# Moving half of the second corner sums of a deformable convolution from Pool to DVE

## The chip, the cores and the metric

The kernel runs on one core of a Trainium2 chip. The metric is the device time of one execution in microseconds, as the median of several runs.

PE is TensorE, DVE is VectorE, ACT is ScalarE, Pool is GpSimd, SP is the engine that issues the loads.

## What is computed

The reference is a chain of eight residual blocks on a tensor x of shape (8, 64, 16, 16), all in float32: multi-scale linear attention, a mixture of experts with two experts per token, a deformable convolution, a feed-forward layer on half of the tokens, a state-space scan along rows, a batch-norm mixture of experts, an involution, and a mixture of experts with one expert per token and a capacity. Each block's input is normalised over channels or tokens.

The change is in the deformable convolution. Two 3x3 convolutions give an offset for each of 4 channel groups and 9 taps, 36 samples per pixel. Each sample is interpolated between four corner pixels, and one product with the weights sums over groups, channels and taps:

```python
val = gather(y0, x0) * (wy0 * wx0)[:, :, None] + gather(y0, x0 + 1) * (wy0 * wx1)[:, :, None] \
    + gather(y0 + 1, x0) * (wy1 * wx0)[:, :, None] + gather(y0 + 1, x0 + 1) * (wy1 * wx1)[:, :, None]
return jnp.einsum('ogck,bgckhw->bohw', wr, val)
```

and `x = x + relu(deform_conv(...))`.

## The kernel before, in words

The kernel holds x in SBUF from start to end and runs the blocks as stages, one after another. Inside a stage each engine has its own instruction list, written out by hand, and semaphores tie the lists together: an instruction increments one when it is done, another engine waits until it has reached a number. The stage of the deformable convolution stands at lines 950 to 1293.

The 2048 pixels (8 images of 256) are 16 tiles of 128 partitions. After the offsets are known, the stage loops over the 36 samples. For one sample `s`:

- SP loads the sample's pixel indices, broadcast to 128 partitions, into one of four buffers `BC` (L1002), as soon as DVE and ACT have used the buffer's former content.
- DVE compares them with the partition's own number (`compare`, L1261), which gives the one-hot matrix `OH` for the lower half of an image. ACT makes `OHU` for the upper half (L1184). Both have three buffers.
- PE gathers the four corners by 64 matmuls with these matrices (`gather`, L1079) into two of four banks of PSUM, alternating with s. It waits for both matrices and, for the bank, for DVE's product of sample s - 2.
- DVE multiplies the gathered corners by the interpolation weights (`weigh`, L1271, two instructions of 128x512) into `U[s % 2]`, which is the tile SQ for even and SD for odd samples. It waits for the gather, and for Pool to be done with `U` of sample s - 2. This pair of instructions is called the product of s.
- Pool adds corners 0 and 1 to corners 2 and 3 (L1015, the first sum, into `V1`) and then the two halves of that (L1018, the second sum, into `VAL`). Samples 0 to 34 are done so; for sample 35 DVE makes both sums itself (L1284, L1285).

DVE's order in the loop is: comparison of s + 1, then product of s. So a comparison runs one sample ahead of its product.

`VAL` has two buffers of eight samples each. When eight samples are summed, PE transposes them (`contract`, L1100, 16 matmuls in four groups, each evicted by ACT, L1177) and later multiplies them by the weights (`project`, L1113). Both stand in PE's list between gathers: `contract` after the gathers of samples 11, 19, 27 and 34, `project` after those of 15, 23 and 31. After the gather of sample 35 follow the last `project` of a full group, the contraction of the last four samples, and their projection. DVE's two last instructions of the stage (L1293) add the result to x.

Pool's loop and DVE's product, with what they wait for:

```python
pool.wait_ge(u_ready, s + 1)
after_pool(pool, pool.tensor_tensor(V1[:, :, :, :], U[s % 2][:, :, 0:2, :], U[s % 2][:, :, 2:4, :], ALU.add))
...
pool.tensor_tensor(VAL[:, (s // 8) % 2, :, s % 8, :], V1[:, :, 0, :], V1[:, :, 1, :], ALU.add).then_inc(val_ready, 1)
pool.wait_ge(val_ready, s + 1)
...
dve.wait_ge(ga_ps, s + 1)
if s >= 2:
    dve.wait_ge(val_ready, s - 1)
```

Three other stages (the mixtures of experts) compute a softmax of gate logits (`softmax_dve`, L736) and use semaphores `g_ps`, `g_exp` and `g_sum` for it, each stage its own three.

Of the kernel before, what the change touches and what calls it, by code (L numbers as in the profile page):

```python
# [12 lines left out]
ALU = mybir.AluOpType  # L13
ACT = mybir.ActivationFunctionType
F32 = mybir.dt.float32
# [5 lines left out]
P = 128  # L21
# [5 lines left out]
TILES = B * PIX // P  # L27
# [7 lines left out]
SAMPLES = 36  # L35
CG = 16
# [39 lines left out]
def build(nc, x_dram, packs, idx_dram, out_dram):  # L76
    with ExitStack() as ctx:
        def sb(name, shape, dt=F32, where=None):
            return (where or ctx).enter_context(nc.sbuf_tensor(name, shape, dt))

        def sem(name):
            return ctx.enter_context(nc.semaphore(name))
# [14 lines left out]
        def wt(name, a=0, n=None, p0=0, p1=P):  # L97
# [10 lines left out]
            "ln_centered", "ln_squared", "ln_var", "ln_sd", "ln_rstd", "ln_spread", "ln_placed", "ln_copied", "ln_done"))  # L108
        TILED = (2, 4, 5)
        dve_step = sem("dve_step")  # L110
        act_step = sem("act_step")
# [18 lines left out]
        def after_pool(eng, ins):  # L130

            steps["pool"] += 1
            ins.then_inc(pool_step, 1)
            eng.wait_ge(pool_step, steps["pool"])
# [115 lines left out]
        with ExitStack() as sctx, nc.Block() as block:  # L250
# [17 lines left out]
            for s in range(1, SCALES):  # L268
# [6 lines left out]
            prepared, ones_set, qkv_ps, qkv_in, t_ps, t_act, t_dve, conv_ps, conv_in, d5_ready, d3_ready = (  # L275
                sem(n) for n in ("prepared", "ones_set", "qkv_ps", "qkv_in", "t_ps", "t_act", "t_dve", "conv_ps", "conv_in",
                                 "d5_ready", "d3_ready"))
# [484 lines left out]
        with ExitStack() as sctx, nc.Block() as block:  # L762
# [11 lines left out]
            HS = sb("HS", [P, 4, HC], F32, sctx)  # L774
            g_ps, g_exp, g_sum, cw_ready, cwt_ps, cwt_in, hid_ps, hid_in, bc_ps, hs_ready, hs_used, cwt3_act, cwt3_dve, cast0, cwt3_ps = (
                sem(n) for n in ("g_ps", "g_exp", "g_sum", "cw_ready", "cwt_ps", "cwt_in", "hid_ps", "hid_in",
                                 "bc_ps", "hs_ready", "hs_used", "cwt3_act", "cwt3_dve", "cast0", "cwt3_ps"))
# [159 lines left out]
        with ExitStack() as sctx, nc.Block() as block:  # L937
# [30 lines left out]
            U = [a[:, :].rearrange("p (t k c) -> p t k c", t=TILES, k=4) for a in (SQ, SD)]  # L968
            V1 = sb("V1", [P, TILES, 2, CG], F32, sctx)
            VAL = sb("VAL", [P, 2, TILES, 8, CG], F32, sctx)  # L970
# [4 lines left out]
                "val_ready", "vt_ps", "vt_in", "dc_ps", "xs_ready"))  # L975
            vt_dve, wc_ready, last_val = sem("s3_vt_dve"), sem("s3_wc_ready"), sem("s3_last_val")

# [29 lines left out]
            @block.gpsimd  # L1007
            def _(pool):
                pool.memset(YP[:, :, :], 0.0).then_inc(y_pad, 1)
                for k in range(3):  # L1010
                    pool.memset(HS3[k][:, :, :], 0.0).then_inc(y_pad, 1)
                for s in range(SAMPLES - 1):

                    pool.wait_ge(u_ready, s + 1)
                    after_pool(pool, pool.tensor_tensor(V1[:, :, :, :], U[s % 2][:, :, 0:2, :], U[s % 2][:, :, 2:4, :], ALU.add))  # L1015
                    if s >= 16 and s % 8 == 0:
                        pool.wait_ge(vt_ps, 4 * (s // 8 - 1))
                    pool.tensor_tensor(VAL[:, (s // 8) % 2, :, s % 8, :], V1[:, :, 0, :], V1[:, :, 1, :], ALU.add).then_inc(val_ready, 1)  # L1018
                    pool.wait_ge(val_ready, s + 1)

            @block.tensor
            def _(pe):
# [60 lines left out]
                def contract(ch):  # L1083

                    ns = min(8, SAMPLES - 8 * ch)
                    rows = ns * CG
                    pe.wait_ge(val_ready, min(8 * ch + ns, SAMPLES - 1))
                    if ch == 4:
                        pe.wait_ge(last_val, 1)
                    for j, q in enumerate(LAST if ch == 4 else range(4)):  # L1090
                        n = 4 * ch + j
                        if n == 19:
                            pe.wait_ge(vt_dve, 1)
                        elif n >= 2:
                            pe.wait_ge(vt_in, n - 1)
                        for i in range(4):

                            t = 4 * (2 * (q % 2) + i // 2) + 2 * (q // 2) + i % 2
                            src = VAL[:, ch % 2, t, 0:ns, :].rearrange("p s c -> p (s c)")
                            mm = pe.transpose(bank(j % 2)[0:rows, i * P:(i + 1) * P], src, wt("ident"))  # L1100
                        mm.then_inc(vt_ps, 1)
                    return rows
# [91 lines left out]
            def _(dve):  # L1194
# [62 lines left out]
                def compare(s):  # L1257
                    dve.wait_ge(bc_in[s % NBC], 16 * (s // NBC + 1))
                    if s >= NOH:
                        dve.wait_ge(ga_ps, s - NOH + 1)  # L1260
                    dve.tensor_scalar(OH[:, s % NOH, :], BC[:, s % NBC, :], wt("qidx"), 0.0625, ALU.is_equal, ALU.mult).then_inc(oh_ready, 1)  # L1261

                def weigh(s):
                    dve.wait_ge(ga_ps, s + 1)
                    if s >= 2:
                        dve.wait_ge(val_ready, s - 1)
                    for half in range(2):
                        o = U[s % 2][:, 8 * half:8 * half + 8, :, :].rearrange("p t k c -> p (t k) c")
                        src = bank(4 + 2 * (s % 2) + half).rearrange("p (k c) -> p k c", c=CG)
                        w = WC[:, s, 8 * half:8 * half + 8, :].rearrange("p t (k o) -> p (t k) o", o=1).broadcast_to([P, 32, CG])  # L1270
                        ins = dve.tensor_tensor(o, src, w, ALU.mult)  # L1271
                    ins.then_inc(u_ready, 1)

                compare(0)
                compare(1)
                dve.wait_ge(wc_ready, NB)
                for s in range(SAMPLES):
                    if 1 <= s < SAMPLES - 1:
                        compare(s + 1)
                    weigh(s)  # L1280
                last = SAMPLES - 1
                sums = PY[:, :, :].rearrange("p t k -> p (t k)")[:, 0:TILES * 2 * CG].rearrange("p (t k c) -> p t k c", k=2, c=CG)
                dve.wait_ge(u_ready, last + 1)
                after(dve, dve.tensor_tensor(sums, U[last % 2][:, :, 0:2, :], U[last % 2][:, :, 2:4, :], ALU.add))  # L1284
                dve.tensor_tensor(VAL[:, (last // 8) % 2, :, last % 8, :], sums[:, :, 0, :], sums[:, :, 1, :], ALU.add).then_inc(last_val, 1)  # L1285
                for j in (1, 3):
# [194 lines left out]
        with ExitStack() as sctx, nc.Block() as block:  # L1481
# [14 lines left out]
            H2W = sb("H2W", [P, H2WBUF, HC], F32, sctx)  # L1496
            (bn_sd, bn_done, sum_done, g_ps, g_exp, g_sum, g_ready, wt_ps, wt_in, wb_ps, wb_in, a_ps, a_in, b_ps, b_in, weighted,
             c_done) = (sem("s6_" + n) for n in (
                "bn_sd", "bn_done", "sum_done", "g_ps", "g_exp", "g_sum", "g_ready", "wt_ps", "wt_in", "wb_ps", "wb_in", "a_ps",
                "a_in", "b_ps", "b_in", "weighted", "c_done"))  # L1500
# [103 lines left out]
            def _(act):  # L1604
# [31 lines left out]
                relu1(1)  # L1636
                act.wait_ge(g_exp, 1)
                act.activation(LG[:, :, :], LG[:, :, :], ACT.Exp).then_inc(g_sum, 1)
# [12 lines left out]
            def _(dve):  # L1651
# [4 lines left out]
                for i in range(2):  # L1656
# [9 lines left out]
                dve.tensor_reduce(SUM[:, :], Y[:, :].rearrange("p (b n) -> p n b", b=NB), AX.X, ALU.add).then_inc(sum_done, 1)  # L1666
                dve.wait_ge(g_ps, 1)
                br = wt("br2").rearrange("p (o e) -> p o e", o=1).broadcast_to([P, 2, E])
                after(dve, dve.scalar_tensor_tensor(out=LG[:, :, :], in0=bank(0, 2 * E).rearrange("p (h e) -> p h e", h=2),
                                                    scalar=1.0 / B, in1=br, op0=ALU.mult, op1=ALU.add))  # L1670
                softmax_dve(dve, LG, RED, 2, g_exp, 1, g_sum)
                dve.wait_ge(lg_zeroed, 1)
# [217 lines left out]
        with ExitStack() as sctx, nc.Block() as block:  # L1890
# [17 lines left out]
            oht_ps, oht_in, x_final = sem("s8_oht_ps"), sem("s8_oht_in"), sem("s8_x_final")  # L1908
            (g_ps, g_exp, g_sum, oh_ready, cum_ps, t_ps, t_in, scale_ready, sc_ps, sc_in, hid_ps, hid_in_a, hid_in_v,
             hid_used) = (sem("s8_" + n) for n in (  # L1910
                "g_ps", "g_exp", "g_sum", "oh_ready", "cum_ps", "t_ps", "t_in", "scale_ready", "sc_ps", "sc_in",
                "hid_ps", "hid_in_a", "hid_in_v", "hid_used"))
# [27 lines left out]
            def _(pe):  # L1940
# [24 lines left out]
                up_w(0)  # L1965
                pe.wait_ge(g_exp, 1)
                up_w(2)
# [63 lines left out]
            def _(act):  # L2031
# [3 lines left out]
                act.wait_ge(ln_done, 16)  # L2035
                act.wait_ge(g_exp, 1)
                act.activation(LG[:, :, :], LG[:, :, :], ACT.Exp).then_inc(g_sum, 1)
# [24 lines left out]
            def _(dve):  # L2062
                ln_dve(dve, 7, flat)
                dve.wait_ge(w_in[8], W_AT[8])
                dve.wait_ge(g_ps, 1)
                for bh in range(2):
# [3 lines left out]
                after(dve, ins)  # L2070
                softmax_dve(dve, LG, RED, TILES, g_exp, 1, g_sum)
                first_max_dve(dve, LG, OTHERS, RED, OH8)
# [307 lines left out]
```

## Time and profile before

| | us |
|---|---|
| median of 3 runs | 561.73 (558.81 to 562.38) |
| the profiled execution | 558.03 |
| its span, from first to last instruction | 556.0 |
| deformable stage, product of sample 0 to product of sample 35 | 226.10 to 317.85 |

The span lies 2.0 us below the profiled execution's own time. The mean granted clock of TensorE over the span is 0.975 of full speed. All rows are of that one execution. A group line of the page has the engine, the operation, the tile written and the tiles read, the shape, the count, then the busy time in us and the mean duration of one instruction in ns, then the idle time of the engine just before these instructions and what ended most of it.

### The profile page before, as it was taken

The numbers are of one execution on the slowest core, as the hardware profiler recorded it, in microseconds if no ns is written. First come the engines' busy times: TensorE is split into PE (matmuls) and PEld (weight loads), VectorE is DVE, ScalarE is ACT, GpSimd is POOL, SyncE is SP. The second block draws the span as 40 slices with busy tenths as digits, with TensorE's granted clock in tenths as the row PEclk, the third lists the DMA queues.
The fourth block names the chain that finished last, engine by engine and source line by source line (L and its number), as shares of the span: only waits on it lengthen the run. The fifth ranks groups of instructions, "written<-read, shape, count | busy, mean of one in ns | idle before, by whom it ended". The sixth has DMA issues, their size and how long they took to land. (4 is left out here: it accounts for less than half of the span.)

```text
span 556.0 us, 12345 instructions
## 1 busy us (share of the span) xinstructions
PE 490.4 (88%) x5281; PEld 253.3 (46%) x5281; DVE 345.6 (62%) x590; ACT 279.6 (50%) x405; POOL 132.0 (24%) x129
## 2 busy tenths in 40 slices
PE   3799998978997999879999979897988898999994
PEld 1344323635222496778888743332324255333331
DVE  2385997467557267677777658666557564763534
ACT  2583223535552136978788447556771552433330
POOL 8080000000003000699999900006102001000000
PEclk9999999998999799999999999988999899999998
DMA  7000000020000002755556000101003000000000
GB/s 290 2 2 2 1 2 1 1 105 6 1 0 34 1 2 93 261 205 212 198 196 212 19 19 2 64 0 46 1 0 123 1 2 2 1 1 0 1 19 19
DMA packets 7990, 29.83 MB, mean 54 GB/s; under 512 B 864, under 2 KB 2176, under 8 KB 7424
## 3 DMA queue, kind: packets, MB, share of 16 engines
q1 hardware_dynamic: 7936, 29.05, 15.0%
q8 instruction: 41, 0.67, 0.5%
q14 instruction: 13, 0.11, 0.1%
HBM read 28.37 MB, written 0.67 MB: 52 GB/s over the span
## 5 line engine op out<-in xcount | busy, mean ns | idle before, releaser
L1079 PE MATMUL PS<-GX,OH 128*128 128x64 f16 x1152 | 70.0, 193 | 9.1 <-DVE OH L1261 9.1
L1184 ACT ACTIVATE OHU<-BC,wbuf 128x2048 fp8e4<-128x2048 f16 x36 | 70.2, 1995 | 11.2 <-PE PS L1079 7.1
L1079 PEld LDWEIGHTS PS<-GX,OH 128*128 128x128 f16 x1152 | 67.5, 98 | 14.0 <-DVE OH L1261 10.4
L1079 PE MATMUL PS<-GX,OHU 128*128 128x64 f16 x1152 | 69.9, 193 | 0.0
L1079 PEld LDWEIGHTS PS<-GX,OHU 128*128 128x128 fp8e4 x1152 | 67.5, 98 | 0.0
L2162 DVE TENSOR_SCALAR HID<-PS,wbuf 128x512 f32<-128x512 f32 x32 | 23.9, 750 | 31.3 <-PE PS L1954 26.4
L2052 ACT ACTIVATE HID<-PS,wbuf 128x512 f32<-128x512 f32 x32 | 21.9, 687 | 39.8 <-PE PS L1954 39.8
L1018 POOL TENSOR_TENSOR VAL<-V 128x256 f32<-128x256 f32 x35 | 40.2, 1147 | 2.7
L695 DVE SCALAR_TENSOR_TENSOR D<-QKVP,wbuf,D 128x1024 f32<-128x1024 f32 x27 | 34.6, 1281 | 7.7 <-ACT D L595 6.9
L426 PE MATMUL PS<-T,DG 128*32 128x512 f32 x336 | 37.1, 594 | 0.0
L1947 PE MATMUL PS<-Y,wbuf 64*128 64x512 f32 x128 | 35.6, 617 | 0.7 <-ACT HID L2052 0.6
L1015 POOL TENSOR_TENSOR V<-SQ 128x512 f32<-128x512 f32 x18 | 24.4, 1354 | 49.6 <-DVE SQ L1271 48.3
L1271 DVE TENSOR_TENSOR SQ<-PS,WC 128x512 f32<-128x512 f32 x36 | 23.2, 686 | 15.1 <-POOL VAL L1018 7.7
L2010 PE MATMUL PS<-HID,wbuf 128*64 128x512 f32 x128 | 30.8, 604 | 0.0
L156 PE MATMUL PS<-X,wconst 128*128 128x512 f32 x32 | 17.4, 671 | 14.4 <-DMA wconst<-pack_dram 7.5
L1271 DVE TENSOR_TENSOR SD<-PS,WC 128x512 f32<-128x512 f32 x36 | 23.2, 684 | 10.7 <-POOL VAL L1018 9.0
L1261 DVE TENSOR_SCALAR OH<-BC,wbuf 128x2048 f16<-128x2048 f16 x36 | 27.9, 774 | 2.0 <-DMA BC<-idx_dram 2.0
L930 DVE TENSOR_TENSOR HS<-PS,HID 128x512 f32<-128x512 f32 x32 | 20.6, 686 | 13.5 <-PE PS L809 13.4
L875 ACT ACTIVATE HID<-PS,wbuf 128x512 f32<-128x512 f32 x32 | 20.2, 684 | 13.4 <-PE PS L800 13.4
L184 ACT ACTIVATE SQ<-PS 128x512 f32<-128x512 f32 x16 | 9.6, 597 | 33.5 <-PE PS L156 25.5
L595 ACT ACTIVATE D<-PS,wbuf 128x512 f32<-128x512 f32 x12 | 8.3, 688 | 28.6 <-PE PS L426 28.6
L800 PE MATMUL PS<-Y,wbuf 64*128 64x512 f32 x64 | 20.7, 689 | 1.5 <-ACT HID L875 1.5
(313 smaller groups left out, 917.0 us busy)
## 6 DMA issues: line engine op xcount, KB each, us to landing
BC<-idx_dram SPq DMA_DIRECT2D x36, 512.0 KB, 4.4
wbuf<-pack_dram SPq DMA_DIRECT2D x1, 1913.0 KB, 9.5
wbuf<-pack_dram SPq DMA_DIRECT2D x1, 1656.0 KB, 7.5
wbuf<-pack_dram SPq DMA_DIRECT2D x1, 1494.0 KB, 6.1
wbuf<-pack_dram SPq DMA_DIRECT2D x1, 1044.0 KB, 11.5
wbuf<-pack_dram SPq DMA_DIRECT2D x1, 871.0 KB, 4.5
wbuf<-pack_dram SPq DMA_DIRECT2D x1, 607.0 KB, 5.4
X<-x_dram SPq DMA_DIRECT2D x2, 256.0 KB, 4.2
```

The lines of the kernel that those rows point to most:

```text
L426: mm = pe.matmul(bank(DBANK[t % 2] + n)[32 * q:32 * q + 32, :], DG[:, (2 * j + hf) * NBLK + i, :], src, start=(i == blocks[0]), stop=(i == ...
L695: ins = dve.scalar_tensor_tensor(out=d, in0=window(QKVP[j], dy, dx), scalar=wt("dw5", j * 25 + 5 * dy + dx, 1), in1=d, op0=ALU.mult, op1=A ...
L1015: after_pool(pool, pool.tensor_tensor(V1[:, :, :, :], U[s % 2][:, :, 0:2, :], U[s % 2][:, :, 2:4, :], ALU.add))
L1018: pool.tensor_tensor(VAL[:, (s // 8) % 2, :, s % 8, :], V1[:, :, 0, :], V1[:, :, 1, :], ALU.add).then_inc(val_ready, 1)
L1079: mm = pe.matmul(o, (OH, OHU)[qh][:, s % NOH, t * P:(t + 1) * P], src, start=(qh == 0 and part == 0), stop=(qh == 1 and part == 1))
L1184: act.activation(OHU[:, s % NOH, :], BC[:, s % NBC, :], ACT.Abs_reciprocal_sqrt, bias=wt("hitq"), scale=HIT, saturate=False).then_inc(uppe ...
L1261: dve.tensor_scalar(OH[:, s % NOH, :], BC[:, s % NBC, :], wt("qidx"), 0.0625, ALU.is_equal, ALU.mult).then_inc(oh_ready, 1)
L1271: ins = dve.tensor_tensor(o, src, w, ALU.mult)
L1947: pe.matmul(bank(2 + (n + bh) % 4), wt("w1_3", e * FH3 + m * P, P, r, r + C), Y[r:r + C, bp * HC:(bp + 1) * HC], start=True, stop=False, t ...
L2010: pe.matmul(bank(bp)[C * bh:C * bh + C, :], wt("w2_3", (2 * e + m) * C, C), HID[:, (n + i) % 8, :], start=(e == 0 and m == 0), stop=(e == ...
L2052: act.activation(HID[:, n % 8, :], bank(2 + n % 4), ACT.Relu, bias=wt("b1_3", 2 * e + m, 1)).then_inc(hid_in_a, 1)
L2162: dve.tensor_scalar(HID[:, n % 8, :], bank(2 + n % 4), wt("b1_3", 2 * e + m, 1), 0.0, ALU.add, ALU.max).then_inc(hid_in_v, 1)
```

## The change

For odd samples 1 to 33 the second sum moves from Pool to DVE (`corner_sum`). DVE does the one of sample s - 2 between the comparison of s + 1 and the product of s, for odd s. Pool keeps all first sums and the second sums of even samples. `V1` becomes two buffers, by the sample's parity, and gets a semaphore of its own, `v1_ready`; DVE's product of s waits for it (first sum of s - 2) instead of `val_ready`. DVE's second sums count on `val_dve`, for which Pool waits before it writes the odd `V1` again. The contractions wait for both counters, half the number of samples each. The sample 35 counts on `val_dve` too, and `last_val` goes.

To make room for the new semaphores, the three mixture stages share one set of `g_ps`, `g_exp` and `g_sum`, and wait for 1, 2 and 3 in turn.

```diff
-            V1 = sb("V1", [P, TILES, 2, CG], F32, sctx)
+            V1 = sb("V1", [P, 2, TILES, 2, CG], F32, sctx)
+            v1_ready, val_dve = sem("s3_v1_ready"), sem("s3_val_dve")
...
                 for s in range(SAMPLES - 1):
 
                     pool.wait_ge(u_ready, s + 1)
-                    after_pool(pool, pool.tensor_tensor(V1[:, :, :, :], U[s % 2][:, :, 0:2, :], U[s % 2][:, :, 2:4, :], ALU.add))
+                    if s >= 3 and s % 2:
+                        pool.wait_ge(val_dve, s // 2)
+                    pool.tensor_tensor(V1[:, s % 2, :, :, :], U[s % 2][:, :, 0:2, :], U[s % 2][:, :, 2:4, :], ALU.add).then_inc(v1_ready, 1)
+                    if s % 2:
+                        continue
+                    pool.wait_ge(v1_ready, s + 1)
                     if s >= 16 and s % 8 == 0:
                         pool.wait_ge(vt_ps, 4 * (s // 8 - 1))
-                    pool.tensor_tensor(VAL[:, (s // 8) % 2, :, s % 8, :], V1[:, :, 0, :], V1[:, :, 1, :], ALU.add).then_inc(val_ready, 1)
-                    pool.wait_ge(val_ready, s + 1)
+                    pool.tensor_tensor(VAL[:, (s // 8) % 2, :, s % 8, :], V1[:, 0, :, 0, :], V1[:, 0, :, 1, :], ALU.add).then_inc(val_ready, 1)
+                    pool.wait_ge(val_ready, s // 2 + 1)
...
-                    pe.wait_ge(val_ready, min(8 * ch + ns, SAMPLES - 1))
-                    if ch == 4:
-                        pe.wait_ge(last_val, 1)
+                    pe.wait_ge(val_ready, (8 * ch + ns) // 2)
+                    pe.wait_ge(val_dve, (8 * ch + ns) // 2)
...
                 def weigh(s):
                     dve.wait_ge(ga_ps, s + 1)
                     if s >= 2:
-                        dve.wait_ge(val_ready, s - 1)
+                        dve.wait_ge(v1_ready, s - 1)
...
+                def corner_sum(s):
+                    dve.wait_ge(v1_ready, s + 1)
+                    if s >= 16 and s % 8 == 1:
+                        dve.wait_ge(vt_ps, 4 * (s // 8 - 1))
+                    dve.tensor_tensor(VAL[:, (s // 8) % 2, :, s % 8, :], V1[:, 1, :, 0, :], V1[:, 1, :, 1, :], ALU.add).then_inc(val_dve, 1)
+
...
                     if 1 <= s < SAMPLES - 1:
                         compare(s + 1)
+                    if s >= 3 and s % 2:
+                        corner_sum(s - 2)
                     weigh(s)
...
-                dve.tensor_tensor(VAL[:, (last // 8) % 2, :, last % 8, :], sums[:, :, 0, :], sums[:, :, 1, :], ALU.add).then_inc(last_val, 1)
+                dve.tensor_tensor(VAL[:, (last // 8) % 2, :, last % 8, :], sums[:, :, 0, :], sums[:, :, 1, :], ALU.add).then_inc(val_dve, 1)
...
-                dve.wait_ge(g_ps, 1)
+                dve.wait_ge(g_ps, 2)
...
-                softmax_dve(dve, LG, RED, 2, g_exp, 1, g_sum)
+                softmax_dve(dve, LG, RED, 2, g_exp, 2, g_sum)
```

## Rows read from the trace of the kernel before

**Rows 1.** The page's costliest groups: PE, ACT and DVE in the stage.

```profile
L1079 PE MATMUL PS<-GX,OH 128*128 128x64 f16 x1152 | 70.0, 193 | 9.1 <-DVE OH L1261 9.1
L1184 ACT ACTIVATE OHU<-BC,wbuf 128x2048 fp8e4<-128x2048 f16 x36 | 70.2, 1995 | 11.2 <-PE PS L1079 7.1
...
L1271 DVE TENSOR_TENSOR SQ<-PS,WC 128x512 f32<-128x512 f32 x36 | 23.2, 686 | 15.1 <-POOL VAL L1018 7.7
...
L1271 DVE TENSOR_TENSOR SD<-PS,WC 128x512 f32<-128x512 f32 x36 | 23.2, 684 | 10.7 <-POOL VAL L1018 9.0
```

**Rows 2.** Busy time by stretch: from:to, length, engines (instructions), clock, DMA share, GB/s.

```profile
257.37:278.41 21.04, 19.48 (x543) 17.37 (x539) 15.85 (x25) 17.64 (x13) 19.79 (x17) 1.00 0.60 203
```

The engines of Rows 2 stand in the order PE matmul, PE weight load, DVE, ACT, Pool.

**Rows 3.** Timeline of Pool: start, duration, line, operation, tiles, shapes, count.

```profile
227.47 1.71 POOL L1015 TENSOR_TENSOR V<-SQ 128x512 f32<-128x512 f32 x1 [48.26 <-DVE SQ L1271]
...
251.74 1.28 POOL L1015 TENSOR_TENSOR V<-SD 128x512 f32<-128x512 f32 x1
253.09 1.21 POOL L1018 TENSOR_TENSOR VAL<-V 128x256 f32<-128x256 f32 x1
254.38 1.28 POOL L1015 TENSOR_TENSOR V<-SQ 128x512 f32<-128x512 f32 x1
...
258.37 0.73 POOL L1018 TENSOR_TENSOR VAL<-V 128x256 f32<-128x256 f32 x1
259.18 1.60 POOL L1015 TENSOR_TENSOR V<-SQ 128x512 f32<-128x512 f32 x1
...
318.36 0.74 POOL L1018 TENSOR_TENSOR VAL<-V 128x256 f32<-128x256 f32 x1
```

**Rows 4.** Timeline of DVE; a product's two instructions are one line.

```profile
226.10 1.29 DVE L1271 TENSOR_TENSOR SQ<-PS,WC 128x512 f32<-128x512 f32 x2 [2.27 <-PE PS L1079]
227.30 0.74 DVE L1261 TENSOR_SCALAR OH<-BC,wbuf 128x2048 f16<-128x2048 f16 x1
227.96 1.28 DVE L1271 TENSOR_TENSOR SD<-PS,WC 128x512 f32<-128x512 f32 x2
...
251.76 1.29 DVE L1271 TENSOR_TENSOR SQ<-PS,WC 128x512 f32<-128x512 f32 x2 [0.70 <-POOL VAL L1018]
...
254.40 1.29 DVE L1271 TENSOR_TENSOR SD<-PS,WC 128x512 f32<-128x512 f32 x2 [0.69 <-POOL VAL L1018]
...
257.37 1.29 DVE L1271 TENSOR_TENSOR SQ<-PS,WC 128x512 f32<-128x512 f32 x2 [1.01 <-PE PS L1079]
258.57 1.08 DVE L1261 TENSOR_SCALAR OH<-BC,wbuf 128x2048 f16<-128x2048 f16 x1
...
317.85 1.29 DVE L1271 TENSOR_TENSOR SD<-PS,WC 128x512 f32<-128x512 f32 x2 [1.68 <-PE PS L1079]
...
319.90 0.42 DVE L1285 TENSOR_TENSOR VAL<-PY 128x256 f32<-128x256 f32 x1
```

**Rows 5.** Timeline of PE: first matmuls of gathers, a contraction and a projection.

```profile
251.12 0.23 PE L1079 MATMUL PS<-GX,OH 128*128 128x64 f16 x2 [0.60 <-DVE OH L1261]
...
253.00 1.07 PE L1100 MATMUL PS<-wconst,VAL 128*128 128x128 f32 x8
...
255.30 0.22 PE L1079 MATMUL PS<-GX,OH 128*128 128x64 f16 x2
...
259.71 0.23 PE L1079 MATMUL PS<-GX,OH 128*128 128x64 f16 x2 [0.52 <-DVE OH L1261]
...
263.55 1.94 PE L1113 MATMUL PS<-VTA,wbuf 128*64 128x512 f32 x8
265.42 0.23 PE L1079 MATMUL PS<-GX,OH 128*128 128x64 f16 x2
```

**Rows 6.** Timelines of a later stage: Pool's scalings, and two additions on DVE.

```profile
383.51 2.92 POOL L1518 TENSOR_SCALAR DGI<-wconst,wbuf 128x128 f32<-128x128 f32 x5
...
384.27 0.21 DVE L739 TENSOR_TENSOR LG<-LG,RED 128x16 f32<-128x16 f32 x1
...
385.16 0.17 DVE L743 TENSOR_TENSOR LG<-LG,RED 128x16 f32<-128x16 f32 x1
```

More of the change, by code:

```diff
@@ L109, in build @@
         TILED = (2, 4, 5)
+        g_ps, g_exp, g_sum = (sem(n) for n in ("g_ps", "g_exp", "g_sum"))
         dve_step = sem("dve_step")
@@ L774, in build @@
             HS = sb("HS", [P, 4, HC], F32, sctx)
-            g_ps, g_exp, g_sum, cw_ready, cwt_ps, cwt_in, hid_ps, hid_in, bc_ps, hs_ready, hs_used, cwt3_act, cwt3_dve, cast0, cwt3_ps = (
-                sem(n) for n in ("g_ps", "g_exp", "g_sum", "cw_ready", "cwt_ps", "cwt_in", "hid_ps", "hid_in",
+            cw_ready, cwt_ps, cwt_in, hid_ps, hid_in, bc_ps, hs_ready, hs_used, cwt3_act, cwt3_dve, cast0, cwt3_ps = (
+                sem(n) for n in ("cw_ready", "cwt_ps", "cwt_in", "hid_ps", "hid_in",
                                  "bc_ps", "hs_ready", "hs_used", "cwt3_act", "cwt3_dve", "cast0", "cwt3_ps"))
@@ L975, in build @@
                 "val_ready", "vt_ps", "vt_in", "dc_ps", "xs_ready"))
-            vt_dve, wc_ready, last_val = sem("s3_vt_dve"), sem("s3_wc_ready"), sem("s3_last_val")
+            vt_dve, wc_ready = sem("s3_vt_dve"), sem("s3_wc_ready")
             bc_in = [sem(f"bc_in{i}") for i in range(NBC)]
@@ L1496, in build @@
             H2W = sb("H2W", [P, H2WBUF, HC], F32, sctx)
-            (bn_sd, bn_done, sum_done, g_ps, g_exp, g_sum, g_ready, wt_ps, wt_in, wb_ps, wb_in, a_ps, a_in, b_ps, b_in, weighted,
+            (bn_sd, bn_done, sum_done, g_ready, wt_ps, wt_in, wb_ps, wb_in, a_ps, a_in, b_ps, b_in, weighted,
              c_done) = (sem("s6_" + n) for n in (
-                "bn_sd", "bn_done", "sum_done", "g_ps", "g_exp", "g_sum", "g_ready", "wt_ps", "wt_in", "wb_ps", "wb_in", "a_ps",
+                "bn_sd", "bn_done", "sum_done", "g_ready", "wt_ps", "wt_in", "wb_ps", "wb_in", "a_ps",
                 "a_in", "b_ps", "b_in", "weighted", "c_done"))
@@ L1636, in _ @@
                 relu1(1)
-                act.wait_ge(g_exp, 1)
+                act.wait_ge(g_exp, 2)
                 act.activation(LG[:, :, :], LG[:, :, :], ACT.Exp).then_inc(g_sum, 1)
@@ L1908, in build @@
             oht_ps, oht_in, x_final = sem("s8_oht_ps"), sem("s8_oht_in"), sem("s8_x_final")
-            (g_ps, g_exp, g_sum, oh_ready, cum_ps, t_ps, t_in, scale_ready, sc_ps, sc_in, hid_ps, hid_in_a, hid_in_v,
+            (oh_ready, cum_ps, t_ps, t_in, scale_ready, sc_ps, sc_in, hid_ps, hid_in_a, hid_in_v,
              hid_used) = (sem("s8_" + n) for n in (
-                "g_ps", "g_exp", "g_sum", "oh_ready", "cum_ps", "t_ps", "t_in", "scale_ready", "sc_ps", "sc_in",
+                "oh_ready", "cum_ps", "t_ps", "t_in", "scale_ready", "sc_ps", "sc_in",
                 "hid_ps", "hid_in_a", "hid_in_v", "hid_used"))
@@ L1965, in _ @@
                 up_w(0)
-                pe.wait_ge(g_exp, 1)
+                pe.wait_ge(g_exp, 3)
                 up_w(2)
@@ L2035, in _ @@
                 act.wait_ge(ln_done, 16)
-                act.wait_ge(g_exp, 1)
+                act.wait_ge(g_exp, 3)
                 act.activation(LG[:, :, :], LG[:, :, :], ACT.Exp).then_inc(g_sum, 1)
@@ L2064, in _ @@
                 dve.wait_ge(w_in[8], W_AT[8])
-                dve.wait_ge(g_ps, 1)
+                dve.wait_ge(g_ps, 3)
                 for bh in range(2):
@@ L2070, in _ @@
                 after(dve, ins)
-                softmax_dve(dve, LG, RED, TILES, g_exp, 1, g_sum)
+                softmax_dve(dve, LG, RED, TILES, g_exp, 3, g_sum)
                 first_max_dve(dve, LG, OTHERS, RED, OH8)
```

## The prediction

> **What bounds the kernel now.** I read the page's costliest groups first [rows 1]. In the deformable stage (lines 950 to 1293) the engines run side by side, and two groups of waits stand out: DVE's products (L1271) wait 7.7 + 9.0 = 16.7 us for Pool's second corner sums, and PE's gathers (L1079) wait 9.1 us for DVE's comparisons. Next I read the stage as stretches of time [rows 2]: from the product of sample 12 to that of sample 20, one round of eight samples in 21.04 us, Pool is busy 19.79 us and PE 19.48 us, at a granted clock of 1.00. Two engines are nearly full, so relieving one may only uncover the other.
>
> Pool's timeline [rows 3] gives the present pace. A first sum (128x512) takes 1.28 us, then come 0.07 us, a second sum (128x256) of 1.21 us and 0.08 us: 254.38 - 251.74 = 2.64 us a sample. DVE's products keep exactly that pace (251.76, 254.40) [rows 4]. A second sum's own work is only 0.73 us (258.37; also 318.36); the other 0.48 us is a comparison on DVE that it runs into. It works the other way too: the comparison at 258.57 began 0.20 us into the second sum of 258.37 and took 1.08 instead of 0.74 us, ending at 259.65, 0.55 us after that sum. And the first sum issued at 259.18 took 1.60 us, ending 1.13 us after that comparison. So Pool's sums and DVE's comparisons exclude each other, in both directions [rows 3, 4].
>
> PE's rows [rows 5] give the rest. A gather begins 0.06 us after its comparison (259.65, then 259.71) and holds PE 253.00 - 251.12 = 1.88 us; the product follows 2.07 us behind the gather's start (255.30, then 257.37). A contraction holds PE 255.30 - 253.00 = 2.30 us, a projection 265.42 - 263.55 = 1.87 us.
>
> **The change part by part.** Removed: 17 second sums of Pool (odd samples 1 to 33), 17 x 1.21 = 20.6 us of Pool's time; and DVE's product of sample s now waits for the first sum of s - 2 alone. Added: 17 second sums on DVE, queued behind a comparison and ahead of a product. The row for it is DVE's own last second sum, 0.42 us (319.90) [rows 4]. The next instruction starts some 0.07 us before such an end (227.96, where the comparison ends at 228.04), which leaves 0.35 us each. The new waits of Pool (for DVE's earlier second sum) and of the contractions (for both counters) are met early: DVE's sum of s - 2 stands ahead of the product of s, for which Pool waits anyway, and the contractions come two or more samples behind the sums they read. They cost nothing; were one late by a whole sum, 0.42 us, the four contractions would lose 1.7 us. The doubled buffer lets an odd first sum be followed at once by the next one. The gate counters shared by other stages change the numbers that are waited for, and no order: nothing.
>
> How the stage then runs I follow through one pair, from the product of an even sample e at time 0 (us):
> - 1.20: DVE begins the comparison of e + 2 (226.10, then 227.30 [rows 4]); it ends at 1.94. Pool's first sum of e, whose products are ready at 1.29, is held by it and ends 1.13 later, at 3.07.
> - 1.86: DVE's corner sum of e - 1 (0.66 after the comparison's start: 227.30, 227.96). 2.21: the product of e + 1. 3.41: the comparison of e + 3.
> - 3.15 to 3.88: Pool's second sum of e. The comparison of e + 3 begins 0.26 us into it, as the one at 258.57 began 0.20 into its own, and so ends 0.55 behind it, at 4.43. The next product starts 0.08 us earlier: the pair takes 4.35.
>
> Pool has 3.3 us of its own work in those 4.35 and bounds nothing. What is late next is a loop that Pool had covered: product, comparison, gather, product two samples on. It takes 1.20 + 0.74 + 0.06 + 2.07 = 4.07 us for two samples with no collision; DVE's own work in a pair (2 x 1.20 + 2 x 0.66 + 0.35 = 4.07) is as long. With the collision it is 4.35, against 5.29 now. 17 such pairs lie between the products of samples 1 and 35.
>
> But in that loop PE's other work no longer hides. At present a gather (251.12) would allow its product at 253.19, and that starts at 254.40; a contraction shows merely as a wait of 1.01 in place of 0.70 us (257.37) [rows 4]. In the new pair the gather of e + 1 holds PE from 0.14 to 2.02 and that of e + 2 from 2.02; its product could start at 4.09 and does at 4.35. A contraction (after samples 11, 19 and 27) moves that gather to 4.32 and the product to 6.39, 2.04 us late; a projection (after 15, 23 and 31) moves them to 3.89 and 5.96, 1.61 late. After sample 34 the gather of 35 waits for a contraction: 2.02 + 1.88 + 2.30 + 2.07 = 8.27 against 6.56, 1.71 late. Together 3 x 2.04 + 3 x 1.61 + 1.71 = 12.7 us. So a round of eight is 4 pairs and 3.65 us, about as long as today, and what is gained is gained ahead of the first contraction. ScalarE (17.64 us busy in a round) and the index loads (0.60 of the DMA engines) [rows 2] have room at that pace.
>
> Does DVE's new sum, with both inputs in SBUF, exclude Pool's sums as a comparison does? No row shows that shape beside Pool. The nearest is an addition with two such inputs that DVE ran while Pool was in the midst of a scaling [rows 6]: 0.21 us, and 0.17 us for the same shape later, so 0.04 us of harm. Five scalings fill 2.92 us from 383.51; the second ends near 384.69, and the addition had ended at 384.48. That is no wait for Pool's instruction to end. I take 0.04 us a pair, as this row is the nearest; the ends are nothing, and a wait for a whole first sum, the second rival.
>
> The Trainium skill speaks against this value. "SBUF — State Buffer", section "Who interferes with whom", says that a DVE instruction with two SBUF inputs contends with a GpSimd instruction that reads SBUF, and that whichever comes second is blocked until the first is done; by it the pair would be 5.09 us. The 0.21 us of that row does not bear out a full block, though at 16 elements it is short and doesn't refute the rule.
>
> **The sum.** 17 x (4.35 + 0.04) = 74.6; plus 12.7; plus 0.4 for the first pair, where Pool's first sum collides at its start (1.71 us [rows 3]): 87.7 us from the product of sample 1 to that of sample 35, where it is now 317.85 - 227.96 = 89.9 [rows 4]. What follows the last product doesn't change. The gain is 2.2 us: 558.03 becomes 555.8 for the profiled execution. The median of the runs, 561.73, lies 3.7 above that; with the same gain it becomes **559.5 us**. The forecast's own range is 558 (the products of rows 3 to 5 with a few hundredths less in each pair) to 563.4 (Pool's and DVE's reads take turns: 256 elements at the pace of the 0.42 us sum, some 0.27 us a pair, so 17 x 0.23 more).
>
> **Rivals.**
> - **Pool's full gain.** If only DVE's work counted and PE's contractions and projections stayed hidden, 17 x 4.07 = 69.2, a gain of 20 us: 541. For it: Pool is the engine that products wait for. Against it: rows 5, by which the loop has no room for that work of PE's.
> - **Blocked corner sums, the slower side.** Place: DVE's corner sum, issued at 1.86, when Pool's first sum, waiting since 1.37, has just been let in. If it must wait for that one's end at 3.07, it ends at about 3.30, the product of e + 1 starts at 3.23, the comparison of e + 3 at 4.43 (no collision), the next product at 5.09. A contraction then costs 1.30 and a projection 0.87, the last contraction nothing: 17 x 5.09 + 3 x 2.17 + 0.4 = 93.4, 3.5 us slower: 565.2. It decides from a wait of about 0.5 us in every pair on. For it: comparisons and Pool's sums do exclude each other [rows 3, 4]. Against it: rows 6.
> - **No collision.** If the comparison of e + 3 comes ahead of Pool's second sum (0.26 us must shift), the pair is 4.07, and with no slack PE's work is added whole: 69.2 + 3 x (2.30 + 1.87) + 1.9 + 0.4 = 84.0, a gain of 5.9: 555.8. Against it: Pool's first sum hangs on the comparison before it, so the order repeats in every pair.
>
> **How the numbers follow.** Forecast 0.56, blocked sums 0.25, no collision 0.14, Pool's full gain 0.03, anything else on the slower side 0.02. A measurement of this kernel tells a change from none at about 1%, 5.6 us. Faster by more: the full gain and most of "no collision", 0.16 with a little of the forecast. Slower by more: "blocked" lies at 0.6%; half of that case and the rest may come out beyond, 0.17. Within 1%: 0.67. The range is 555.5 to 567: "no collision" at the low end, "blocked" and some 2 us that the order of the two engines may add at the high end.
>
> **What would show it.** Pool's busy time in the stage falls by about 17 us. Before the first contraction products come in pairs of about 4.4 us (5.1 if blocked, 4.1 without collision), and every second comparison takes about 1.05 us. The waits of products for Pool vanish and waits for PE take their place, over 2 us behind a contraction. A corner sum of over 1 us on DVE means the block. If rounds of eight samples fall below 19 us, the loop is not the bound, and this prediction is wrong.

## The result, and the profile after

The changed kernel took 568.84 us in the median of four runs (565.43 to 570.15), the kernel before 561.57 beside it: a ratio of 1.0148, with a 95% interval of 1.0109 to 1.0186. Ratios here and below leave out executions in a slower state and can differ a little from the quotient of the two medians, here 1.013. The forecast was 559.5 with a range of 555.5 to 567.0. It was on the wrong side and out of its range. Two later measurements of the same kernel (below) gave 1.0051 and 1.0073, so part of the 1.5% didn't repeat.

First, the profiled execution by stretch, before and after; the columns are those of [rows 2], and the third line of each is the time from the product of sample 1 to that of sample 35. The kernel before:

```profile
14.00:28.00 14.00, 11.21 (x108) 5.50 (x115) 4.35 (x6) 7.10 (x11) 1.17 (x2) 1.00 0.01 2
28.00:227.96 199.96, 185.00 (x1646) 90.46 (x1630) 132.87 (x223) 90.31 (x150) 17.22 (x18) 0.97 0.08 27
227.96:317.85 89.89, 80.59 (x2266) 73.07 (x2268) 66.42 (x103) 72.42 (x49) 84.56 (x69) 1.00 0.52 180
317.85:556.00 238.15, 208.38 (x1251) 82.52 (x1251) 138.79 (x257) 106.36 (x190) 17.28 (x27) 0.96 0.06 18
```

The kernel after (gathers now stand at L1086, first sums at L1019, Pool's second sums at L1025, comparisons at L1267, products at L1277, DVE's new sums at L1284):

```profile
14.00:28.00 14.00, 11.25 (x44) 5.80 (x52) 2.95 (x3) 5.39 (x8) 1.07 (x2) 0.76 0.00 1
28.00:230.27 202.27, 186.90 (x1710) 90.94 (x1710) 134.61 (x226) 91.96 (x153) 17.22 (x18) 0.98 0.08 26
230.27:324.59 94.32, 80.83 (x2266) 73.19 (x2268) 86.66 (x119) 72.10 (x49) 71.79 (x53) 1.00 0.50 172
324.59:568.00 243.41, 214.83 (x1251) 84.00 (x1251) 138.70 (x257) 106.42 (x190) 16.62 (x26) 0.94 0.05 17
```

Samples 1 to 35 take 94.32 us, 4.43 more than before, at a granted clock of 1.00 in both. (The one other profile with the stage of before, that of the additions beside scalings below, has 89.86 us.) Pool is relieved there by 12.8 us, DVE gets 20.2 more. The other 7.6 us of the two spans (568.0 and 556.0) lie outside: 2.3 ahead of sample 1 and 5.3 behind sample 35, where the change has no work beyond the renumbered gate counters, and where the granted clock was lower in places (0.76 against 1.00 from 14 to 28 us).

The costliest groups of the page after, against [rows 1]:

```profile
L1086 PE MATMUL PS<-GX,OH 128*128 128x64 f16 x1152 | 70.2, 193 | 13.3 <-DVE OH L1267 11.5
...
L1019 POOL TENSOR_TENSOR V<-SD 128x512 f32<-128x512 f32 x17 | 27.5, 1616 | 12.2 <-DVE SD L1277 12.1
...
L1277 DVE TENSOR_TENSOR SQ<-PS,WC 128x512 f32<-128x512 f32 x36 | 23.1, 682 | 8.2 <-PE PS L1086 8.2
...
L1284 DVE TENSOR_TENSOR VAL<-V 128x256 f32<-128x256 f32 x17 | 24.4, 1433 | 0.0
L1277 DVE TENSOR_TENSOR SD<-PS,WC 128x512 f32<-128x512 f32 x36 | 23.0, 677 | 1.4 <-PE PS L1086 1.4
```

The products' 16.7 us of waits for Pool are gone, and now Pool waits for DVE (12.1 us). The line that differs from the forecast is L1284: 17 corner sums fill 24.4 us of DVE, where the forecast had 17 x 0.46 (0.42 and 0.04 of harm). Their timeline on DVE, columns as in [rows 4]:

```profile
239.11 0.74 DVE L1267 TENSOR_SCALAR OH<-BC,wbuf 128x2048 f16<-128x2048 f16 x1
239.77 1.49 DVE L1284 TENSOR_TENSOR VAL<-V 128x256 f32<-128x256 f32 x1
241.18 1.27 DVE L1277 TENSOR_TENSOR SD<-PS,WC 128x512 f32<-128x512 f32 x2
242.38 0.74 DVE L1267 TENSOR_SCALAR OH<-BC,wbuf 128x2048 f16<-128x2048 f16 x1
243.04 1.28 DVE L1277 TENSOR_TENSOR SQ<-PS,WC 128x512 f32<-128x512 f32 x2
...
259.69 1.29 DVE L1277 TENSOR_TENSOR SQ<-PS,WC 128x512 f32<-128x512 f32 x2 [1.18 <-PE PS L1086]
...
322.73 0.42 DVE L1284 TENSOR_TENSOR VAL<-V 128x256 f32<-128x256 f32 x1
324.59 1.29 DVE L1277 TENSOR_TENSOR SD<-PS,WC 128x512 f32<-128x512 f32 x2 [1.44 <-PE PS L1086]
```

And on Pool, against [rows 3]:

```profile
239.27 1.71 POOL L1019 TENSOR_TENSOR V<-SQ 128x512 f32<-128x512 f32 x1
241.05 0.80 POOL L1025 TENSOR_TENSOR VAL<-V 128x256 f32<-128x256 f32 x1
...
322.83 1.45 POOL L1019 TENSOR_TENSOR V<-SQ 128x512 f32<-128x512 f32 x1
```

Pool's first sum is issued at 239.27, into the comparison that ends at 239.85, and ends 1.13 later (240.98), as in [rows 3]. DVE's corner sum, issued at 239.77, is by then the second in line: it ends at 241.26, 0.28 behind Pool's sum, and has taken 1.49 us for work of 0.42. The last corner sum has no comparison ahead of it and is issued 0.10 us before Pool's first sum (322.73, 322.83). Then the roles change: it takes 0.42 us, and Pool's sum takes 1.45, ending at 324.28, again 1.13 behind the end of DVE's instruction. So the two exclude each other, and the first one in keeps the other out. The total agrees: 16 x 1.50 + 0.42 = 24.4.

A pair of samples takes 3.27 + 1.86 = 5.13 us (237.91 to 243.04 on DVE). That is no more than the 2 x 2.64 us before. The loss shows where PE has other work, which Pool's pace had hidden: a pair with a contraction takes 6.38 us (253.31 to 259.69), one with a projection 6.05, so 1.25 and 0.92 us more, three times each. 17 x 5.13 + 3 x 2.17 makes 93.7 of the 94.3 us.

### The profile page after: what moved, and what is told of

The parts are those of the page before. It is cut to its first block and busy times, and to the rows that moved or that the text cites. A ratio compares the mean times of both kernels' runs of the same rounds, so it can differ in the third digit from the quotient of the medians.

```text
span 568.0 us, 12332 instructions
## 1 busy us (share of the span) xinstructions
PE 498.5 (88%) x5281; PEld 255.5 (45%) x5281; DVE 365.8 (64%) x607; ACT 279.2 (49%) x405; POOL 118.6 (21%) x112
## 5 line engine op out<-in xcount | busy, mean ns | idle before, releaser
L1086 PE MATMUL PS<-GX,OH 128*128 128x64 f16 x1152 | 70.2, 193 | 13.3 <-DVE OH L1267 11.5
L1086 PEld LDWEIGHTS PS<-GX,OH 128*128 128x128 f16 x1152 | 67.5, 98 | 18.3 <-DVE OH L1267 13.6
L1086 PE MATMUL PS<-GX,OHU 128*128 128x64 f16 x1152 | 70.1, 193 | 0.0
L1086 PEld LDWEIGHTS PS<-GX,OHU 128*128 128x128 fp8e4 x1152 | 67.5, 98 | 0.0
L1019 POOL TENSOR_TENSOR V<-SQ 128x512 f32<-128x512 f32 x18 | 30.6, 1698 | 57.2 <-DVE SQ L1277 55.9
L1961 PE MATMUL PS<-Y,wbuf 64*128 64x512 f32 x128 | 36.5, 632 | 0.7 <-ACT HID L2066 0.6
L157 PE MATMUL PS<-X,wconst 128*128 128x512 f32 x32 | 19.1, 728 | 14.7 <-DMA wconst<-pack_dram 7.7
L1019 POOL TENSOR_TENSOR V<-SD 128x512 f32<-128x512 f32 x17 | 27.5, 1616 | 12.2 <-DVE SD L1277 12.1
L1267 DVE TENSOR_SCALAR OH<-BC,wbuf 128x2048 f16<-128x2048 f16 x36 | 27.0, 749 | 2.4 <-DMA BC<-idx_dram 2.4
L1277 DVE TENSOR_TENSOR SQ<-PS,WC 128x512 f32<-128x512 f32 x36 | 23.1, 682 | 8.2 <-PE PS L1086 8.2
L1284 DVE TENSOR_TENSOR VAL<-V 128x256 f32<-128x256 f32 x17 | 24.4, 1433 | 0.0
L1277 DVE TENSOR_TENSOR SD<-PS,WC 128x512 f32<-128x512 f32 x36 | 23.0, 677 | 1.4 <-PE PS L1086 1.4
```

Of the source, the lines that this page charges most:

```text
L1019: pool.tensor_tensor(V1[:, s % 2, :, :, :], U[s % 2][:, :, 0:2, :], U[s % 2][:, :, 2:4, :], ALU.add).then_inc(v1_ready, 1)
L1086: mm = pe.matmul(o, (OH, OHU)[qh][:, s % NOH, t * P:(t + 1) * P], src, start=(qh == 0 and part == 0), stop=(qh == 1 and part == 1))
L1284: dve.tensor_tensor(VAL[:, (s // 8) % 2, :, s % 8, :], V1[:, 1, :, 0, :], V1[:, 1, :, 1, :], ALU.add).then_inc(val_dve, 1)
L1961: pe.matmul(bank(2 + (n + bh) % 4), wt("w1_3", e * FH3 + m * P, P, r, r + C), Y[r:r + C, bp * HC:(bp + 1) * HC], start=True, stop=False, t ...
```

## The experiments

Theory: the block of the corner sum is the whole loss; without it the stage runs as the forecast said. Rivals: the 0.74 us by which a pair is above the forecast (5.13 against 4.39) come from DVE's place in the loop whatever its input is, or from the relaxed wait and the changed gate counters.

**One input instead of two.** The corner sum as a reduction over one tensor:

```diff
-    dve.tensor_tensor(VAL[:, (s // 8) % 2, :, s % 8, :], V1[:, 1, :, 0, :], V1[:, 1, :, 1, :], ALU.add)
+    dve.tensor_reduce(VAL[:, (s // 8) % 2, :, s % 8, :], V1[:, 1, :, :, :].rearrange("p t k c -> p t c k"), AX.X, ALU.add)
```

> DVE's corner sum is made as a reduction over the pair of halves: the same sums from the same tile, but one input tensor in place of two. Theory (two inputs in SBUF wait for Pool's first sum): a corner sum takes about 0.7 us instead of 1.50, the pair of samples about 4.4 us instead of 5.13, product of sample 1 to product of sample 35 about 88 us (changed kernel 94.3, before 89.9); whole time within 1% of before. Rival (the sum waits for something else, such as the count of the first sums arriving late): still about 1.5 us and 5.1 us a pair, whole time 1 to 1.5% above before.

Measured: 558.56 us, ratio 0.9948 (0.9913 to 0.9983). DVE's timeline:

```profile
239.43 1.28 DVE L1277 TENSOR_TENSOR SQ<-PS,WC 128x512 f32<-128x512 f32 x2
240.63 0.74 DVE L1267 TENSOR_SCALAR OH<-BC,wbuf 128x2048 f16<-128x2048 f16 x1
241.29 0.69 DVE L1284 TENSOR_REDUCE VAL<-V 128x256 f32<-128x512 f32 x1
241.90 1.27 DVE L1277 TENSOR_TENSOR SD<-PS,WC 128x512 f32<-128x512 f32 x2
243.09 0.78 DVE L1267 TENSOR_SCALAR OH<-BC,wbuf 128x2048 f16<-128x2048 f16 x1
243.79 1.28 DVE L1277 TENSOR_TENSOR SQ<-PS,WC 128x512 f32<-128x512 f32 x2
...
255.82 1.29 DVE L1277 TENSOR_TENSOR SQ<-PS,WC 128x512 f32<-128x512 f32 x2 [2.22 <-PE PS L1086]
...
266.24 1.29 DVE L1277 TENSOR_TENSOR SQ<-PS,WC 128x512 f32<-128x512 f32 x2 [1.62 <-PE PS L1086]
```

Pool:

```profile
240.78 1.71 POOL L1019 TENSOR_TENSOR V<-SQ 128x512 f32<-128x512 f32 x1
242.57 0.74 POOL L1025 TENSOR_TENSOR VAL<-V 128x256 f32<-128x256 f32 x1
```

The reduction takes 0.68 to 0.70 us, the whole stage long, at the same place behind the same comparisons. It begins and ends inside Pool's first sum (241.29 to 241.98 in 240.78 to 242.49), in 16 of the 17 cases. The pair is 243.79 - 239.43 = 4.36, the forecast's 4.35 (there from a sum of 0.42 and a comparison of 1.05; here 0.69 and 0.78). That isn't luck: the comparison ends 0.56 us behind Pool's second sum (243.31, 243.87), as the forecast had it (0.55), and a longer sum ahead of it only starts it later. The three waits behind a contraction are 2.22, 1.60 and 1.95 us and those behind a projection 1.62 to 1.63, where the forecast had the products 2.04 and 1.61 late. Samples 1 to 35 take 317.49 - 228.20 = 89.29 us, 1.6 above the 87.7 of the forecast and 1.3 above what was expected of this run. PE stood still for 1.00 us in the gather of sample 9 (until 245.82) and for 1.11 in that of sample 18 (until 271.28), for which the profile shows no releaser, and the products of these samples waited 0.83 and 0.91 us for PE; that is about the difference. The place in the loop is not the cause of the long sums; the next run separates the second input from the operation.

**An input from PSUM.** The same addition, its first input read from the gather's bank in PSUM, the memory that PE writes to; the odd second sums then hold other numbers.

```diff
+    dve.wait_ge(ga_ps, s + 3)
-    dve.tensor_tensor(VAL[...], V1[:, 1, :, 0, :], V1[:, 1, :, 1, :], ALU.add)
+    dve.tensor_tensor(VAL[...], bank(6, 256).rearrange("p (t c) -> p t c", c=CG), V1[:, 1, :, 1, :], ALU.add)
```

> DVE's corner sum takes its first input from the gather's bank in PSUM instead of from the first sum's tile (so the odd second sums hold other numbers: this part of the computation is changed); operation, size and place are the same. Theory (two inputs in SBUF): 0.42 us, pair about 4.4 us, product 1 to product 35 about 88 us. Rival: about 1.5 us and 5.1 us as in the changed kernel.

Measured: sums of 0.42 us, samples 1 to 35 in 88.82 us, 560.03 us, ratio 0.9956 (0.9912 to 1.0001). DVE:

```profile
254.40 0.42 DVE L1285 TENSOR_TENSOR VAL<-PS,V 128x256 f32<-128x256 f32 x1 [0.35 <-PE PS L1086]
```

Pool's first sum runs from 253.47 to 255.18 meanwhile, and 15 of the 17 sums lie inside one like this. The same operation with the same number of elements isn't blocked once only one of its inputs is in SBUF. So it is the second input in SBUF that blocks it.

**The other order.** The corner sum ahead of the comparison:

```diff
+    if s >= 3 and s % 2:
+        corner_sum(s - 2)
     if 1 <= s < SAMPLES - 1:
         compare(s + 1)
-    if s >= 3 and s % 2:
-        corner_sum(s - 2)
```

> The corner sum stands ahead of the comparison instead of behind it. Theory (exclusion): the sum gets in ahead of Pool's next first sum and takes 0.42 us, but now the comparison finds Pool's first sum running and takes up to 1.9 us instead of 0.74, a pair 5 us or more, whole time 1 to 2.5% above before. Rival (a late count): the sum is as long as before, the comparison 0.74 us.

Measured: 566.63 us, ratio 1.0117 (1.0064 to 1.0169); samples 1 to 35 in 96.91 us. DVE:

```profile
236.84 0.41 DVE L1284 TENSOR_TENSOR VAL<-V 128x256 f32<-128x256 f32 x1
237.17 1.75 DVE L1267 TENSOR_SCALAR OH<-BC,wbuf 128x2048 f16<-128x2048 f16 x1
238.84 1.28 DVE L1277 TENSOR_TENSOR SD<-PS,WC 128x512 f32<-128x512 f32 x2
```

Pool:

```profile
237.00 1.37 POOL L1019 TENSOR_TENSOR V<-SQ 128x512 f32<-128x512 f32 x1 [0.52 <-DVE SQ L1277]
```

Now the sum comes first and is short, Pool's first sum is let in behind it (237.25 + 1.12 = 238.37), and the comparison pays, ending at 238.92, 0.55 behind Pool as in [rows 3, 4]. The price has only changed its payer, and it is higher: a gather waits for the comparison, products wait 0.28 us for PE in every pair, and a pair takes 5.43 us.

**The sum behind the product.** `corner_sum(s - 2)` moved below `weigh(s)`.

> The corner sum with two inputs stands behind the odd sample's product instead of behind the comparison. Theory (exclusion: what counts is what Pool is doing when the sum is issued): the sum meets Pool's short second sum or an idle Pool, is short of 1 us, and the stage is about 90 us, whole time within 0.5% of before. Rival (a sum on DVE costs 1.5 us beside Pool wherever it stands): 94 us and more, whole time about 1% above before.

Measured: sums of 0.42 to 0.74 us, samples 1 to 35 in 90.02 us, 559.92 us, ratio 0.9983 (0.9948 to 1.0019). Behind the product the sum meets Pool's second sum (Pool: 238.51, 0.73 us; the corner sum ends at 239.52, again 0.28 behind it), the last hundredths of a first sum, or nothing, and the loss of the stage is gone without any change of the operation.

**The relaxed wait alone.** Pool makes all second sums again, in `V1` of two buffers, and DVE's product waits for the first sum only:

```diff
-    if s >= 3 and s % 2:
-        pool.wait_ge(val_dve, s // 2)
...
-    if s % 2:
-        continue
...
-    if s >= 3 and s % 2:
-        corner_sum(s - 2)
```

> Only the waits and the second buffer of the change: Pool makes all second sums again, DVE none, and DVE's product waits for the first sum alone. Theory: Pool sets the pace as before, 2.64 us a sample, product 1 to product 35 about 90 us, whole time within 0.3% of before. If the shared gate counters or the doubled buffer cost anything outside the stage, the rest of the kernel is slower here too.

Measured: 557.54 us, ratio 0.9947 (0.9916 to 0.9977), samples 1 to 35 in 88.11 us. That no gain was expected was a miss. DVE:

```profile
237.49 1.38 DVE L1264 TENSOR_SCALAR OH<-BC,wbuf 128x2048 f16<-128x2048 f16 x1
```

Pool:

```profile
237.04 1.28 POOL L1017 TENSOR_TENSOR V<-SQ 128x512 f32<-128x512 f32 x1
238.40 1.07 POOL L1021 TENSOR_TENSOR VAL<-V 128x256 f32<-128x256 f32 x1
239.55 1.28 POOL L1017 TENSOR_TENSOR V<-SD 128x512 f32<-128x512 f32 x1
```

DVE reaches its comparison while Pool's first sum runs, so it is already waiting when that ends (238.32 + 0.55 = 238.87), and Pool's second sum is held up for less: 1.07 in place of 1.21 us, and 2.51 a sample in place of 2.64 ahead of the first contraction. It also acquits the gate counters, which this kernel has as the changed one does.

**Comparisons two samples ahead.** The loop product, comparison, gather, product is cut by `compare(s + 2)`, in three kernels: with the reduction, with the relaxed wait alone, and with the change as it is.

```diff
-    if 1 <= s < SAMPLES - 1:
-        compare(s + 1)
+    if s < SAMPLES - 2:
+        compare(s + 2)
```

> DVE's comparisons run two samples ahead of the products instead of one, on top of the corner sum with one input. Theory (the loop product, comparison, gather, product sets the pace of about 4.36 us a pair, and PE's contractions and projections are added whole because a gather can't run ahead): the loop is cut, waits for PE behind contractions shrink, product 1 to product 35 falls from 89.3 to about 84 us, whole time about 1% below before. Rival (DVE's own work, or the exclusion with Pool, sets the pace): 88 us or more, whole time as with one sample ahead.

Measured: 554.79 us, ratio 0.9897 (0.9848 to 0.9946); samples 1 to 35 in 84.03 us. This beats both kernels.

> The same on top of the kernel with the waits alone (Pool makes all second sums). Theory: Pool's sums (2.0 us of their own and the comparisons they exclude) bound it near 2.5 us a sample, product 1 to 35 about 86 us, whole time 0.4 to 0.9% below before. Rival (the loop was not what bounded): 88 us, as with one sample ahead.

Measured: 556.19 us, ratio 0.9927 (0.9898 to 0.9957); 85.09 us.

> The changed kernel, corner sum with two inputs, with comparisons two samples ahead. Theory: the sums stay blocked at about 1.5 us and the pair at 5.1, but behind contractions and projections nothing more is lost, so product 1 to 35 is about 90 us and the whole time within 0.5% of before. Rival (the loop is cut, so the block no longer shows): 85 us.

Measured: 561.11 us, ratio 1.0009 (0.9970 to 1.0047); 90.99 us. DVE:

```profile
255.28 1.49 DVE L1284 TENSOR_TENSOR VAL<-V 128x256 f32<-128x256 f32 x1
256.69 1.27 DVE L1277 TENSOR_TENSOR SD<-PS,WC 128x512 f32<-128x512 f32 x2
257.89 0.74 DVE L1267 TENSOR_SCALAR OH<-BC,wbuf 128x2048 f16<-128x2048 f16 x1
259.65 1.29 DVE L1277 TENSOR_TENSOR SQ<-PS,WC 128x512 f32<-128x512 f32 x2 [1.03 <-PE PS L1086]
```

With the block in place, cutting the loop brings 94.3 - 91.0 = 3.3 us; without it 89.3 - 84.0 = 5.3. Between the two kernels that cut it, the block alone makes 91.0 - 84.0 = 7.0 us. And against the relaxed wait alone, the unblocked move of the sums brings nothing as the loop stands (89.29 against 88.11) and 1.1 us once it is cut (84.03 against 85.09).

**Additions beside scalings.** To see why [rows 6] misled, the kernel before got four additions of 256 elements of two tiles in SBUF, on DVE while Pool scales (and four of 16 elements, 0.60 us together):

```diff
+    after(dve, dve.memset(TRY[:, 0:2, :], 1.0))
+    for k in range(4):
+        dve.tensor_tensor(TRY[:, 2 + k, :], TRY[:, 0, :], TRY[:, 1, :], ALU.add)
...
```

> The kernel before, with eight additions of two SBUF tiles (four of 256 and four of 16 elements, their results unused) put on DVE in the later stage where Pool runs its 18 scalings and DVE has nothing to do. It is a measurement of the row on which the prediction took its 0.04 us. Theory (such an addition waits for Pool's running instruction, whatever it is): single additions of 256 elements take 0.6 us and more instead of 0.42 and end where Pool's instructions end; Pool's scalings are stretched too. Rival (Pool's scalings, with one input and 128 elements, hold the port for a small part of their 0.60 us): 0.42 to 0.5 us, 0.17 to 0.21 us for 16 elements.

One execution (561.65 us). DVE:

```profile
387.38 0.42 DVE L1677 TENSOR_TENSOR TRY<-TRY 128x256 f32<-128x256 f32 x1
387.72 0.59 DVE L1677 TENSOR_TENSOR TRY<-TRY 128x256 f32<-128x256 f32 x1
388.24 0.41 DVE L1677 TENSOR_TENSOR TRY<-TRY 128x256 f32<-128x256 f32 x1
388.57 0.58 DVE L1677 TENSOR_TENSOR TRY<-TRY 128x256 f32<-128x256 f32 x1
```

Pool:

```profile
387.44 0.83 POOL L1519 TENSOR_SCALAR DGI<-wconst,wbuf 128x128 f32<-128x128 f32 x1
388.25 0.86 POOL L1519 TENSOR_SCALAR DGI<-wconst,wbuf 128x128 f32<-128x128 f32 x1
...
389.70 0.60 POOL L1519 TENSOR_SCALAR DGI<-wconst,wbuf 128x128 f32<-128x128 f32 x1
```

Two of the four additions took 0.42 us and two 0.58 and 0.59, so neither the theory nor the rival held throughout. Scalings and additions do get in each other's way. A scaling issued just behind an addition ends 0.47 or 0.46 us after it (387.80 to 388.27, 388.65 to 389.11), and the next addition ends 0.04 us after that scaling, where a corner sum ended 0.28 after Pool's first sum. So the scaling kept the addition out until about 0.28 - 0.04 = 0.24 us before its own end: it holds what they share for part of its 0.60 us, and costs an addition at most 0.17 us (0.59 - 0.42). How long it is held is an estimate, not shown directly; the first addition agrees with it, as it was issued 0.08 us before the end of a scaling (386.86, 0.60 us) and took 0.42.

**The changed kernel again**, twice, twelve executions each, on two chips, no edit.

> The changed kernel itself once more. Theory (all of the loss is the stage's, 94.3 against 89.9 us from product 1 to product 35): 0.6 to 1.0% above before. Rival (the change costs something outside the stage too, as the 7.3 us of the first measurement and a lower mean clock would have it): again 1.3% or more, with the same places at a low clock in the profile.

> The changed kernel a third time, since its first measurement (1.5% above before) and its second (0.5%) differ by more than their intervals, with the same stage of 94.3 us in both profiles. If the loss is the stage's alone: 0.4 to 1.0% above before. If something outside the stage belongs to the change: 1.3% or more.

Measured: 563.48 us, ratio 1.0051 (1.0019 to 1.0084), and 563.81, ratio 1.0073 (1.0033 to 1.0113). Samples 1 to 35 took 94.29 and 94.32 us, corner sums 24.3 us in both. From 14 to 28 us the granted clock was 1.00 in the one and 0.88 in the other; over the whole executions it was 0.973 and 0.972 in the mean of twelve, against 0.961 to 0.968 in the first measurement's four. So the loss of the stage, 4.4 us or 0.8%, repeats to a few hundredths and lies in both intervals, which stay below 1.3%; the further 0.7% of the first measurement came with a lower clock elsewhere and didn't repeat. What lowered it there was not settled.

## Why the prediction was wrong

- **What bounds the kernel: right.** Two nearly full engines, and a loop that Pool had covered. With Pool relieved and no block (the reduction), products wait for PE behind every contraction and projection (1.60 to 2.22 us), and 14 us less of Pool's busy time (70.27 in place of 84.56) bring 0.6 us. Cutting the loop brings 5 more.
- **"I take 0.04 us a pair, as this row is the nearest": the step that failed.** The corner sum beside Pool's first sum cost 1.49 - 0.42 = 1.07 us, 16 times. The row was near in operation (an addition of two inputs in SBUF) and far in what decides, the neighbour: a scaling cost an addition of the corner sum's size at most 0.17 us, a first sum 1.07. The 0.04 itself compares two additions that both ran beside Pool's five scalings (383.51 to 386.43), at 384.27 and 385.16, so it wasn't measured against an undisturbed one. And the argument "That is no wait for Pool's instruction to end" took the end of the instruction for the end of the exclusion; by the estimate from the additions beside scalings these differ by 0.24 us there.
- **The rival "Blocked corner sums": it happened as written,** at its place, for its reason. Pair 5.13 (5.09 forecast), every comparison but one 0.74 or 0.75 us with no collision, contraction and projection 1.25 and 0.92 us on top of the pair (1.30 and 0.87), samples 1 to 35 in 94.3 us (93.4). Its 3.5 us were 4.4: the sum ended 0.28 instead of 0.23 us behind Pool's and the pair was 0.04 longer, which makes 0.7 in 17 pairs; most of the rest is the first pair (230.27 to 236.05, 5.78 us). It had a chance of 0.25, and the rows on comparisons and Pool's sums, which the text itself set against [rows 6], were the closer ones, since they have the same neighbour.
- **The Trainium skill had it right for these sums.** "SBUF — State Buffer", section "Who interferes with whom", was cited for a full block of the second to come and set aside. The corner sums (1.49 us behind, 0.42 ahead) bear it out; the scalings, by the estimate above, hold an addition off for only part of their 0.60 us. The same section says that a DVE instruction with at most one SBUF input, outside the modes in which it uses two SBUF ports, doesn't contend: the reduction (0.68 to 0.70 us throughout) and the PSUM input (0.42) agree. The comparisons read one tensor and do exclude Pool's sums; whether they run in such a mode no run here shows.
- **The range:** its high end stood some 2 us above the rival. The first measurement lies 1.8 above that, with a lower clock outside the stage, which had no place in the working; the two later ones (563.5, 563.8) lie inside, but on the slower side.
- **"Pool's busy time in the stage falls by about 17 us":** it fell by 12.8, since 35 first sums now take 58.1 us, most of them 1.6 to 1.7 each, held by DVE.
- **The relaxed wait, given no price of its own:** it is worth 1.8 us alone (88.11 against 89.89), as it lets the comparison wait behind the first sum instead of running into the second.

## What to carry to other kernels

Where two engines exclude each other, take the price from a row with the same neighbour, and ask who is first in line: here an addition on DVE with two inputs in SBUF paid the rest of Pool's 128x512 addition (1.07 us), and beside a small scaling at most 0.17. Work moved from Pool to DVE wants a form that isn't blocked (here a reduction, or an operand in PSUM) or a place where Pool is idle. One SBUF input alone is no warrant: the comparisons have one and are blocked. And in this kernel even the unblocked move brought more than the relaxed wait alone only once the loop behind Pool was cut as well. The stage's own time repeated to hundredths where the whole kernel moved by a per cent, so read the change there first.

## What was not expected of the hardware

A Pool addition of 128x512 with two inputs ends 1.11 to 1.16 us after the DVE instruction that held it, whether that is a comparison or a corner sum, and in the other direction a corner sum that had to wait ends 0.27 to 0.30 and a comparison 0.54 to 0.57 us after Pool, in every run here: near enough to constants that a whole round can be laid out from them. A scaling on Pool keeps a DVE addition out for only part of its 0.60 us (an estimate, above). Executions of one kernel differ in their mean granted clock, and longer times tend to go with a lower one: in the third measurement of the changed kernel 0.962 went with 568.2 us, 0.978 and 0.981 with 560.6 and 560.7; the first had 0.961 to 0.968 with 565.4 to 570.2.
